# Routed rows that carry their home row: expert results scattered tile by tile, plain loads in place of sixteen gathers

## What is computed

```python
logits = x @ gate_w.T
scores = softmax(logits)
topk_w, topk_i = top_k(scores, 2)
topk_w = topk_w / (topk_w.sum(-1) + 1e-20) * 2.5
g = silu(x @ w_gate[e]) * (x @ w_up[e])          # for each expert e
expert_out = g @ w_down[e]
y = sum over the token's two experts of topk_w * expert_out
return y + silu(x @ sw_gate) * (x @ sw_up) @ sw_down
```

## Time and profile before

| | |
|---|---|
| median of 3 runs | 1319.09 us |
| the 3 runs | 1308.81, 1319.09, 1319.71 us |
| profiled execution, its own time | 1315.18 us |
| its span (first to last instruction) | 1313.4 us |
| mean granted TensorE clock | 0.945 of full speed |
| TensorE busy in the span | 90% |

### The profile page before, as it was taken

The page is one execution under the profiler, slowest core; times in us unless marked ns, Lnnn a source line. Parts: engine busy times, 40 slices in busy tenths (PEclk is TensorE's granted clock), DMA queues, the critical chain, the costliest instruction groups (busy, mean ns, idle before and its releaser), DMA issues. The chain is left out here.

```text
span 1313.4 us, 32379 instructions
## 1 busy us (share of the span) xinstructions
PE 1181.7 (90%) x13863; PEld 1040.6 (79%) x13863; DVE 691.2 (53%) x1100; ACT 572.9 (44%) x943; POOL 404.4 (31%) x357
## 2 busy tenths in 40 slices
PE   4799999999999999999999999877796999378799
PEld 4789989989989989989899887665674777266588
DVE  6555655655655655655655633256562221564732
ACT  4465555555555555555555662235521222111500
POOL 5632432432332332332332333245152000423000
PEclk9899999999999999999999997687898999689999
DMA  6937747747647747647647633083021111315055
GB/s 199 212 79 170 162 86 170 163 87 176 157 88 173 158 87 175 156 89 177 154 93 170 137 77 92 18 299 155 1 89 68 46 60 57 93 52 213 2 182 192
DMA packets 63141, 164.62 MB, mean 125 GB/s; under 512 B 25032, under 2 KB 38424, under 8 KB 59928
## 3 DMA queue, kind: packets, MB, share of 16 engines
q1 hardware_dynamic: 60312, 157.32, 47.3%
q0 software_dynamic: 1536, 4.20, 0.9%
q10 hardware_dynamic: 1152, 1.05, 0.2%
HBM read 72.66 MB, written 10.48 MB: 63 GB/s over the span
## 5 line engine op out<-in xcount | busy, mean ns | idle before, releaser
L453 ACT ACTIVATE xa_pt<-xa_sc 128x1024 f32<-128x1024 f32 (+1 forms) x224 | 212.3, 962 | 124.7 <-PE xa_sc L671 124.5
L499 DVE TENSOR_REDUCE xa_mx<-xa_sc 128x2 f32<-128x804 f32 x256 | 243.7, 991 | 43.0 <-PE xa_sc L655 43.0
L671 PE MATMUL xa_sc<-xa_queries,xa_keys 104*128 104x128 f32 (+1 forms) x1664 | 229.5, 282 | 2.5 <-DVE xa_queries L514 1.8
L671 PEld LDWEIGHTS xa_sc<-xa_queries,xa_keys 104*128 104x128 f32 (+1 forms) x1664 | 203.7, 193 | 20.8 <-issue 7.9
L580 PE MATMUL xa_pj<-xa_ctx_hi,xa_wk 128*128 128x400 f32 (+1 forms) x512 | 157.3, 349 | 1.0 <-DVE xa_qst L527 0.9
L580 PE MATMUL xa_pj<-xa_wv,xa_ctx_hi 128*128 128x256 f32 (+1 forms) x832 | 155.1, 285 | 0.1
L682 PE MATMUL xa_op<-xa_pt,xa_values 128*32 128x64 f32 x6656 | 141.7, 228 | 8.4 <-ACT xa_pt L453 3.9
L655 PE MATMUL xa_sc<-xa_keys,xa_queries 96*128 96x402 f32 x512 | 134.7, 365 | 11.6 <-DMA xa_keys<-xa_kst_hi 7.1
L335 POOL TENSOR_TENSOR xa_ctx_lo<-xa_raw,xa_ctx_hi 128x1600 fp32r<-128x1600 f32 (+1 forms) x32 | 115.9, 3622 | 78.0 <-DVE xa_ctx_hi L492 75.4
L340 POOL TENSOR_TENSOR xa_kst_lo<-xa_wk,xa_kst_hi 128x400 fp32r<-128x400 f32 x64 | 67.2, 1050 | 228.2 <-ACT xa_kst_hi L407 228.0
L580 PEld LDWEIGHTS xa_pj<-xa_wv,xa_ctx_hi 128*128 128x128 f32 (+1 forms) x832 | 126.1, 184 | 7.9 <-issue 6.3
(11 more groups left out here) (317 smaller groups left out, 1751.9 us busy)
## 6 DMA issues: line engine op xcount, KB each, us to landing
xa_keys<-xa_kst_hi SPq DMA_DIRECT2D x256, 200.2 KB, 6.1
xa_keys<-xa_kst_lo SPq DMA_DIRECT2D x128, 200.2 KB, 5.5
xa_raw<-in_ctxT SPq DMA_DIRECT2D x15, 1601.0 KB, 9.3
gf_w<-in_gf_w SPq DMA_DIRECT2D x16, 1024.0 KB, 7.1
moe_ex<-in_moe_ex SPq DMA_DIRECT2D x8, 1088.0 KB, 14.6
xa_queries<-xa_qst SPq DMA_DIRECT2D x96, 32.0 KB, 4.3
moe_slots_in<-in_moe_zero SPq DMA_DIRECT2D x1, 2944.0 KB, 17.5
moe_xs<-moe_slots_in SPq DMA_DIRECT2D x23, 128.0 KB, 2.2
```

The lines of the kernel that those rows point to most:

```text
L453: nc.scalar.activation(PT[ptslot(step)][0:rows, 0:nt], SC[bank(step)][0:rows, 0:nt], ACT.Exp, scale=float(D0) ** -0.5).then_inc(ex_done, 1)
L499: nc.vector.tensor_reduce(mx[:, u // 2, 2 * (u % 2):2 * (u % 2) + 2], SC[bank(step)][:, :, 0:MXN], AX.X, ALU.max).then_inc(mx_done, 1)
L671: last = mm(SC[bank(step)][0:rows, kk, a * P:(a + 1) * P], KS[:, 2 * a + h, kt * P:kt * P + rows], QS[b % 2][:, 2 * a + h, :], start=True, ...
```

## The change

Each routed row becomes ROW = 258 numbers long: the 256 of y, in column HOME twice the token's number, and in column LAST its second place. From these VectorE computes, for each tile of expert results, the rows of a new tensor YH (`moe_home_rows`, 39 x 128 rows) to which its rows belong: row 2 x token for the token's first place, 2 x token + 1 for its second. Rows that no token fills go to rows of their own behind them; XG is filled for that from a new input (`empty`) with rows of 258 numbers instead of zeros. GpSimd scatters each tile's result to YH as soon as it is there, and SyncE brings YH back in 4 plain loads, 2 KB for each token. NYS becomes 3.

```diff
-NXS, NYS, NYG = 5, 2, 4
+NXS, NYS, NYG = 5, 3, 4
+ROW, HOME, LAST = D + 2, D, D + 1
...
-    loads += [(XG.rearrange("(i p) d -> p i d", p=P), w["zero"].unsqueeze(1).to_broadcast([P, NT, D]), w_in)]
+    loads += [(XG.rearrange("(i p) d -> p i d", p=P), w["empty"], w_in)]
...
 SyncE
-            for i in range(NT + NXS):
-                if i < NT:
-                    if i >= NXS:
-                        sp.wait_ge(xt_full, i - NXS + 1)
-                    sp.dma_start(XS[i % NXS][:], XG[i * P:(i + 1) * P]).then_inc(xs_in[i % NXS], 16)
-                n = i - NXS
-                if n >= 0:
-                    sp.wait_ge(y_ev, n + 1)
-                    sp.dma_start(YG[n * P:(n + 1) * P], YS[n % NYS][:]).then_inc(y_out[n % NYS], 16)
+            for i in range(NT):
+                if i >= NXS:
+                    sp.wait_ge(xt_full, i - NXS + 1)
+                    sp.wait_ge(homed, i - NXS + 1)
+                sp.dma_start(XS[i % NXS][:], XG[i * P:(i + 1) * P]).then_inc(xs_in[i % NXS], 16)
+            for j in range(NYS):
+                sp.wait_ge(y_out[j], 16 * len(range(j, NT, NYS)))
+            step = T // NYG
+            for g in range(NYG):
+                sp.dma_start(ex[:, 2 * step * D * g:2 * step * D * (g + 1)].rearrange("p (t n) -> p t n", t=step),
+                             YH[2 * step * P * g:2 * step * P * (g + 1)].rearrange("(t p k) d -> p t (k d)", p=P, k=2)).then_inc(gathered[g], 16)
...
 GpSimd
-                                                 in_=y[:, t], in_offset=None).then_inc(scattered, 16)
-            for j in range(NYS):
-                pool.wait_ge(y_out[j], 16 * len(range(j, NT, NYS)))
-            for t in range(T):
-                for k in range(2):
-                    nc.gpsimd.indirect_dma_start(out=back[2 * t + k], out_offset=None, in_=YG,
-                                                 in_offset=bass.IndirectOffsetOnAxis(ap=idx[:, k, t:t + 1], axis=0)).then_inc(gathered[t * NYG // T], 16)
+                                                 in_=rows[:, t], in_offset=None).then_inc(scattered, 16)
+            for i in range(NT):
+                pool.wait_ge(homed, i + 1)
+                pool.wait_ge(y_ev, i + 1)
+                nc.gpsimd.indirect_dma_start(out=YH, out_offset=bass.IndirectOffsetOnAxis(ap=home[:, i:i + 1], axis=0),
+                                             in_=YS[i % NYS][:], in_offset=None).then_inc(y_out[i % NYS], 16)
...
 VectorE: scores(), places(), step xt, the sums at the end
+                step_(V.tensor_copy(rows[:, :, HOME], token))
...
+                step_(V.tensor_copy(rows[:, :, LAST], p2[:, 1]))
                 V.tensor_copy(idx[:], p2[:]).then_inc(placed, 1)
...
                     V.tensor_copy(XT[i % 2][:], XP).then_inc(xt_ev, 1)
+                    xs = XS[i % NXS]
+                    V.scalar_tensor_tensor(home[:, i:i + 1], xs[:, LAST:LAST + 1], place[:, i:i + 1], xs[:, HOME:HOME + 1],
+                                           ALU.is_equal, ALU.add).then_inc(homed, 1)
...
-                    dve.wait_ge(gathered[t * NYG // T], 16 * 2 * T // NYG)
+                    dve.wait_ge(gathered[t * NYG // T], 16)
...
 program(): the layer norm writes y into rows of 258
-        y = moe_stack.enter_context(nc.sbuf_tensor("moe_y", [P, T, D], f32))
+        rows = moe_stack.enter_context(nc.sbuf_tensor("moe_rows", [P, T, ROW], f32))
-        layer_norm(nc, 2, ln, X, stats, lnT, c, also=splits[4], y=y)
+        layer_norm(nc, 2, ln, X, stats, lnT, c, also=splits[4], y=rows[:, :, 0:D])
```

More of the change, by code:

```diff
@@ L1199 @@
 NT = (T * P * TOPK) // P + NE - 1
-NXS, NYS, NYG = 5, 2, 4
+NXS, NYS, NYG = 5, 3, 4
+ROW, HOME, LAST = D + 2, D, D + 1
 def expert_buffers(nc, ctx, w):
     sb = lambda n, s: ctx.enter_context(nc.sbuf_tensor(f"moe_{n}", s, f32))
-    ex, gate, mc = sb("ex", [P, NE * WE]), sb("gate", [P, CH, NE]), sb("consts", [P, 2 * P + NT])
+    ex, gate, mc = sb("ex", [P, NE * WE]), sb("gate", [P, CH, NE]), sb("consts", [P, 2 * P + NT + NT + T])
     raw = [ex[:, (NE - 2 + j) * WE:(NE - 1 + j) * WE] for j in range(2)]
@@ L1210, in expert_buffers @@
     w_in = ctx.enter_context(nc.semaphore("moe_w_in"))
-    XG, YG = [nc.dram_tensor(f"moe_{n}", (NT * P, D), f32, kind="Internal").ap() for n in ("slots_in", "slots_out")]
+    XG = nc.dram_tensor("moe_slots_in", (NT * P, ROW), f32, kind="Internal").ap()
+    YH = nc.dram_tensor("moe_home_rows", ((2 * T + NT) * P, D), f32, kind="Internal").ap()
     loads = [(gate[:], w["gate"], w_in), (mc[:], w["consts"], w_in)]
     loads += [(gu[j], w["sgu"][j], w_in) for j in range(2)] + [(dn[j], w["sdown"][j], w_in) for j in range(2)]
-    loads += [(XG.rearrange("(i p) d -> p i d", p=P), w["zero"].unsqueeze(1).to_broadcast([P, NT, D]), w_in)]
+    loads += [(XG.rearrange("(i p) d -> p i d", p=P), w["empty"], w_in)]
     routed = [(ex[:, e * WE:(e + 1) * WE], w["ex"][e], w_in) for e in range(NE)]
     loads += routed[:NE - 2]
-    return (ex, gate, mc, gu, dn, w_in, 16 * len(loads), XG, YG, routed[NE - 2:]), loads
+    return (ex, gate, mc, gu, dn, w_in, 16 * len(loads), XG, YH, routed[NE - 2:]), loads
 def shared_splits(nc, ctx, buffers, rows_done):
@@ L1258, in expert_order, with experts @@
     return o + down(1)
-def experts(nc, tag, X, y, stats, lnT, c, buffers, splits):
+def experts(nc, tag, X, rows, stats, lnT, c, buffers, splits):
     ctx = ExitStack()
@@ L1266, in experts @@
         sem = lambda n: ctx.enter_context(nc.semaphore(f"{tag}_{n}"))
-        ex, gate, mc, _, _, w_in, loaded, XG, YG, last_experts = buffers
+        ex, gate, mc, _, _, w_in, loaded, XG, YH, last_experts = buffers
         gu, dn, w_lo, low_part, _ = splits
-        strict, ones, slots = mc[:, 0:P], mc[:, P:2 * P], mc[:, 2 * P:]
+        strict, ones, slots = mc[:, 0:P], mc[:, P:2 * P], mc[:, 2 * P:2 * P + NT]
+        place, token = mc[:, 2 * P + NT:2 * P + 2 * NT], mc[:, 2 * P + 2 * NT:]
         lg, sc8, pk = [sb(n, [P, T, NE]) for n in ("lg", "sc8", "pk")]
@@ L1282, in experts @@
         at_ = sb("at", [P, NT], mybir.dt.int32)
+        home = sb("home", [P, NT], mybir.dt.int32)
         h = [sb(f"h{k}", [P, 3, T * P], f32r) for k in range(2)]
@@ L1286, in experts @@
         h32 = [sb(f"h32{j}", [P, 512]) for j in range(2)]
-        XS = [sb(f"xs{j}", [P, D]) for j in range(NXS)]
+        XS = [sb(f"xs{j}", [P, ROW]) for j in range(NXS)]
         XT = [sb(f"xt{j}", [P, CH, P]) for j in range(2)]
@@ L1307, in experts @@
         dn_full, dn_read, xt_full, xt_ev, ht_full, ht_ev, y_ev = [sem(x) for x in ("dn_full", "dn_read", "xt_full", "xt_ev", "ht_full", "ht_ev", "y_ev")]
-        scattered = sem("scattered")
+        scattered, homed = sem("scattered"), sem("homed")
         xs_in = [sem(f"xs_in{j}") for j in range(NXS)]
@@ L1844, in program @@
         moe_stack = ExitStack()
-        moe = {k: a["moe_" + k] for k in ("gate", "sgu", "sdown", "ex", "consts", "zero")}
+        moe = {k: a["moe_" + k] for k in ("gate", "sgu", "sdown", "ex", "consts", "empty")}
         expert_parts, expert_loads = expert_buffers(nc, moe_stack, moe)
@@ L1854, in program @@
             self_attention(nc, "sa", att, X, stats, lnT, c, W, w_in, row, H0, D0, D0, c["quarter"], rope=True, loads=expert_loads, early=(early_qk, early_done))
-        y = moe_stack.enter_context(nc.sbuf_tensor("moe_y", [P, T, D], f32))
+        rows = moe_stack.enter_context(nc.sbuf_tensor("moe_rows", [P, T, ROW], f32))
         splits = shared_splits(nc, moe_stack, expert_parts, (ln["norm"], sum(LN_TILES[:3])))
-        layer_norm(nc, 2, ln, X, stats, lnT, c, also=splits[4], y=y)
-        experts(nc, "moe", X, y, stats, lnT, c, expert_parts, splits)
+        layer_norm(nc, 2, ln, X, stats, lnT, c, also=splits[4], y=rows[:, :, 0:D])
+        experts(nc, "moe", X, rows, stats, lnT, c, expert_parts, splits)
         moe_stack.close()
@@ L1927, in slot_constants, with empty_rows @@
     slots = np.tile(np.arange(NT, dtype=np.float32)[None], (P, 1))
-    return np.concatenate([strict, np.ones((P, P), np.float32), slots], 1)
+    place = np.arange(NT)[None] * P + p[:, None]
+    token = 2 * (np.arange(T)[None] * P + p[:, None])
+    return np.concatenate([strict, np.ones((P, P)), slots, place, token], 1).astype(np.float32)
+def empty_rows():
+    import numpy as np
+    rows = np.zeros((P, NT, ROW), np.float32)
+    rows[:, :, HOME] = 2 * T * P + np.arange(NT)[None] * P + np.arange(P)[:, None]
+    rows[:, :, LAST] = -1.0
+    return rows
 def kernel(**inputs):
@@ L1995 @@
         "moe_consts": slot_constants(),
-        "moe_zero": np.zeros((P, D), np.float32),
+        "moe_empty": empty_rows(),
         "mc_w1": rows(W[:, :D].T), "mc_w2": rows(W[:, D:].T), "mc_b": i["L1_xattn_b"],
```

## The result

The changed kernel takes 1310.80 us (median of 20 runs, 1302.86 to 1316.25), the kernel before 1316.31 us (median of 20 in the same comparison, 1308.81 to 1323.45). The ratio is 0.9959, with a 95% interval of 0.9943 to 0.9975: 5.4 us less, between 3.3 and 7.5. The profiled execution took 1311.57 us with a span of 1309.8.

What follows compares the result with a forecast made beforehand. The gathers' issue rate was taken to set the end of the sums, where TensorE stands idle. Removing VectorE's waits gains 7.9 us, copies cost 0.2: 1317.1 - 7.7 = 1309.4, say 1309 us, range 1299 to 1321.

Steps and rivals of the forecast that it cites:

- base of 1317.1: Starting time of the forecast: middle of the profiled execution and three timed runs of the kernel before.
- The gathers' rate sets the end, and 7.9 us go: Sums after the expert tiles: VectorE idles before each pair for gathers every 1.27 us; without them 7.9 us are gained.
- From the last tile to the loads: End of the tile loop: last scatter lands 2.4 us from its start, loads issued at about 1117.4, all in time.
- Scatter for each tile: nothing: Tile loop: 23 scatters of 0.96 us on idle GpSimd, one per 4.22 us tile, cost nothing.
- SyncE's queue: nothing: XG loads in the loop: 23 stores leave the queue, a wait for `homed` comes in; no cost.
- VectorE: 0.2 us: 23 small instructions covered by idle time in the loop; two strided copies in the routing cost 0.2 us, bounds 0 to 0.5.
- Rows of 1032 bytes: Layer norm, XG fill and sixteen scatters with rows of 258 numbers: taken as 0, upper bound 15 us on the scatters.
- A: Rival at the sums: the four loads come late, VectorE waits, 3 to 4 us of gain lost, 1313 us; chance 0.10.
- B: Rival in the tile loop: scatters delay TensorE's signals beyond 3.0 us, costing 20 us, 1329 us; chance 0.07.
- C: Rival at the sixteen scatters to XG: longer rows lengthen each issue, 1317 us, at the upper bound 1324; chance 0.08.
- E: Rival at the block's end: something else, SyncE's or GpSimd's end, sets it; chance almost nothing.
- D: Rival at the sixteen scatters to XG: TensorE's stall there goes or shrinks, 8.3 us more gained, 1301 us; chance 0.15.

Runs made afterwards that it cites:

- home rows with gathers: Changed kernel with sixteen indirect gathers of the home rows in place of the four plain loads: 1308.80 us, ratio 1.0029 to the kernel before.
- first pair of traces: Profiles of the kernel before and the changed kernel, one execution each, on a chip with the stall: 1315.18 and 1311.57 us.
- third comparison: Changed kernel unaltered, rerun beside the kernel before on a chip without the stall: 1293.14 us against 1299.88, ratio 0.9956.
- three scatters: Changed kernel with each expert tile scattered three times, once home and twice to spare tensors nobody reads: 1305.36 us in one run.
- eight gathers: Kernel before with eight gathers in place of sixteen, each token's first row used twice, so VectorE's work is the same: 1296.93 us, ratio 0.9919.
- filled hole: Changed kernel with 50 unread matmuls behind the last shared product and 5 before the layer norm's transposes: 1299.62 us, ratio 0.9945 to the kernel before.
- one load: Changed kernel with one plain load of 2 MB in place of four of 512 KB: 1300.12 us, ratio 0.9978 to the kernel before.
- first comparison: Pause, three scatters, one load and 48 filler matmuls, each on the changed kernel, beside the kernel before (1303.46 us) on one chip.
- version with a pause: Changed kernel with the sixteen scatters to XG in two halves and a wait between: 1301.09 us, ratio 0.9980 to the kernel before.

## Why the prediction was right, point by point

The forecast was 1309, the median is 1310.8, and the sign and the reason held. That the level came out so close is partly luck: the base of 1317.1 was 0.8 us above the median of the kernel before and hid a part of what the gain was too large by, and the level belongs to a chip with the stall. On two chips without it the changed kernel took 1297.23 and 1293.14 us, below the range of 1299 to 1321. What can be compared from chip to chip is the gain. Against the kernel before of the same comparison the forecast gain of 7.7 us met 5.4 (3.3 to 7.5), 6.9 (3.0 to 10.8) and 5.7 (1.8 to 9.7).

- **The gathers' rate sets the end, and 7.9 us go.** Shown from both sides: with gathers put back the idle times return (home rows with gathers), and with half the gathers alone they go. TensorE's hole shrank by 8.3 us in the first pair of traces and by 8.9 in the third comparison, where the first idle time was 1.79 and not 1.13 us.
- **From the last tile to the loads.** Forecast 2.4 us from the start of the scatter to its landing; it took 3.4 (1116.79 to 1120.18), and 3.0 to 3.8 in the other traces with one scatter for each tile. The forecast also had no term from ScalarE's end to the scatter's start, 0.8 us (1116.03 to 1116.79). The loads went out 2.8 us later than forecast, 1.1 of them because the last tile itself came later in this execution. The four loads took 5.1 us each in the median, near the 5.5 of the forecast, but VectorE can start on the first 3.8 us behind its issue (three scatters). By that estimate it was there at about 1124.0, and VectorE wanted it at 1124.87. No cost, but less than 1 us to spare at the first group. The others had more: no load took over 6.5 us and the last was issued at about 1121.6, so all had landed by 1128.1, where the forecast had 1132.0.
- **Scatter for each tile: nothing.** True in the loop, even threefold. Between the eight gathers and the change TensorE's idle time differs by 0.1 us.
- **SyncE's queue: nothing.** The loads from XG take 2.0 us to landing (2.2 in the earlier trace rows), and TensorE is busy through the whole loop.
- **VectorE: 0.2 us.** One of the two strided copies took 1.30 us, beside a GpSimd operation of 1.28 that began with it. But the first scatter came 39.34 us behind the layer norm's start against 39.30, so it cost nothing.
- **Rows of 1032 bytes.** Sixteen scatters of 0.96 us each, as before. The fill of XG takes 22.3 us in place of 17.5, hidden, as forecast.
- **What the sum lacked** is a term for TensorE's clock. It counted TensorE's work as fixed, and only the idle time as gain. In the third comparison 8.6 us of idle time went and 4.6 us of work came. In the pair at the top it is 8.8 and 5.2. By the ratios the forecast gain was missed by 0.8 to 2.3 us, less than the two pairs of traces say. That such a term exists is likely from the traces together and from the mean clocks. That the hole brings it, and no other part of the change, fits the trace of the eight gathers (1185.9 us of work without any other part of the change), but not the mean clock of their six executions. The filled hole doesn't decide it: what it won was lost to a wait. So the size of the term, some 1 to 5 us, and its cause stay open.
- **Rivals.** A (loads late) came only when made, with one load or with three scatters. B (scatters hold up the loop) is refuted for one scatter a tile in the profile at the top, where the stall is, and for three on a chip without it; the rule of the Trainium skill, "SBUF — State Buffer", section "SBUF: two separate sides", by which TensorE and ScalarE wait on nobody for SBUF, agrees with the loop's rows (88.00 of 88.00 us busy). The prediction took from it that nothing in the loop could be held up, which is more than it says: VectorE shares a port pair with GpSimd. The late signals of the sixteen scatters stay unexplained by it. C (longer rows) didn't happen. E didn't. D (the stall goes) was wrong as put: the change does nothing to it. In the stage of the experts TensorE idles 7.5 us longer in the kernel before at the top than in the one of the third comparison (38.20 and 30.67 us), and 7.6 us longer in the changed one (29.25 and 21.62). Nor is the spread of the kernel before a sign of a stall that comes and goes: it is as wide where no trace has one (1295.84 to 1310.56 us in the first comparison), and goes with the mean granted clock (0.955 in the shortest of these, 0.941 in the longest). The stall was in three of the fourteen traces, twice in the kernel before and once in the changed one, and in no trace of the three comparisons whose kernel before took 1300 to 1305 us; where it was, the kernel before took 1316. So it comes with the chip or its condition, as far as 14 traces can say, and not with the change. What it is stays open: only its place is shown, the stretch of the sixteen scatters, and the version with a pause never ran where it occurs.

## What to carry to other kernels

Where an engine waits at a steady rhythm for a queue that issues by the piece (here 1.27 us a gather, 16 pieces), put the irregular addressing where the queue has time, in the loop (0.96 us of scatter in turns of 4.22), and leave plain loads in a few groups for the tail. When idle time of TensorE goes away, the gain can be less than its length: compare TensorE's work for the same matmul count before and after, and book the difference as a term of the sum. And before a stall in one trace is given a cause, look at it on a second chip.

## What was not expected of the hardware

- In the stretch of the sixteen scatters VectorE idled 7.08, 9.84 and 10.61 us for TensorE's signal in three traces, and 1.4 us on three other chips at the same rate of scatters. TensorE's idle time in the stage of the experts was 7.5 to 9.5 us longer for it.
- Filling TensorE's hole kept the granted clock at 1.00 in it and behind it and shortened that stage by 1.9 us, and the whole was no faster: the next stage, at 0.90 with and without the filling, idled 1.7 us longer.
- A VectorE copy of 128 x 8 numbers took 1.30 us beside a GpSimd operation that began with it, and a like one 0.17 us alone.
- An indirect scatter of 128 rows holds GpSimd for 0.96 us with 0.30 between two, at 1024 or 1032 bytes a row. What waited for the last one's landing came 2.4 us behind its start for the sixteen to XG, and 3.0 to 3.8 us at the end of the loop.
